# A scan whose sum trails by three units, and a quantised layer spread over more slots

## The reference

```python
deltaA = jnp.exp(delta[..., None] * A)
deltaBu = delta[..., None] * Bm[:, :, None, :] * u_bld[..., None]
h = dA * h + dBu                     # along the 512 positions
y = jnp.einsum('bdn,bn->bd', h, c)   # sum over the 16 states
```

```python
s = jnp.maximum(jnp.sqrt(jnp.maximum(amax_x, EPS) / jnp.maximum(amax_w, EPS)), EPS)
xs = x / s
ws = w * s
x_scale = jnp.maximum(jnp.max(jnp.abs(xs), axis=-1, keepdims=True), EPS) / QMAX
x_q = jnp.clip(jnp.round(xs / x_scale), -QMAX, QMAX)   # and w_q likewise
return x_q @ w_q.T * x_scale * w_scale.T
```

## Time and profile before

| what | value |
|---|---|
| median of 3 runs | 5994.26 us (5991.43 to 5997.09) |
| the profiled execution | 5995.06 us, of which the span is 5993.5 us |
| busy: PE, DVE, ACT, POOL | 4792.9, 3930.6, 2807.4, 2208.3 us |
| the scan, first recurrence to last weighing | 68.5 to 700 us |
| norm of phase 2 | 704 to 732 us |
| the eight jobs of the quantised layer | 735 to 952 us |
| phases 3 to 6 | from 953 us to the end |

### The profile page before, as it was taken

One profiled execution on the slowest core, in us unless ns is written; L12 is line 12 of the kernel. 1 busy time (PEld: TensorE's weight loads), 2 busy tenths in 40 slices (PEclk: granted clock), 3 DMA queues, 4 the chain that ended last, 5 costly groups with the idle time before them and its releaser, 6 DMA issues. The chain is left out here.

```text
span 5993.5 us, 81416 instructions
## 1 busy us (share of the span) xinstructions
PE 4792.9 (80%) x24371; PEld 3098.5 (52%) x24457; DVE 3930.6 (66%) x6523; ACT 2807.4 (47%) x5085; POOL 2208.3 (37%) x2728
## 2 busy tenths in 40 slices
PE   6788747999568888888888888888888665888857
PEld 4556534556335655655565555655655332444423
DVE  5667664322357877777777777777777244888757
ACT  5565352111034555555545555555555213777733
POOL 3455400110234554545545445455455044000100
PEclk8899877999789999999999999999999787999989
DMA  2101005244431111111111111111110044111110
GB/s 61 29 29 29 15 29 195 75 146 152 140 98 51 41 41 50 41 54 46 49 45 41 52 52 46 43 39 49 45 47 27 11 138 143 54 53 54 44 62 24
DMA packets 355942, 365.92 MB, mean 61 GB/s; under 512 B 100528, under 2 KB 253616, under 8 KB 354320
## 3 DMA queue, kind: packets, MB, share of 16 engines
q1 hardware_dynamic: 335856, 286.73, 15.9%
q0 software_dynamic: 19744, 74.99, 3.6%
HBM read 264.76 MB, written 96.86 MB: 60 GB/s over the span
## 5 line engine op out<-in xcount | busy, mean ns | idle before, releaser
L1915 POOL TENSOR_TENSOR delta_rule_suffix<-delta_rule_suffix,delta_rule_prefix 128x256 f32<-128x256 f32 x448 | 511.4, 1142 | 1088.0 <-ACT delta_rule_prefix L2016 841.2
L2300 PE MATMUL delta_rule_level<-delta_rule_qk_second,delta_rule_k_first 128*128 128x128 f32 x3072 | 444.8, 289 | 174.4 <-DVE delta_rule_L_small L2108 105.3
L2300 PEld LDWEIGHTS delta_rule_level<-delta_rule_qk_second,delta_rule_k_first 128*128 128x128 f32 x3072 | 384.4, 196 | 257.0 <-DVE delta_rule_qk_second L2119 165.2
L2276 PE MATMUL delta_rule_proj<-delta_rule_hT,delta_rule_w_qkv 128*128 128x512 f32 x1024 | 467.5, 600 | 0.0
L311 POOL TENSOR_TENSOR scan_hc<-scan_hs,scan_c_rows 128x512 f32<-128x512 f32 x256 | 334.5, 1312 | 283.6 <-DVE scan_hs L478 267.9
L2177 DVE TENSOR_TENSOR delta_rule_prefix<-delta_rule_prefix 128x256 f32<-128x256 f32 x448 | 326.5, 729 | 171.1 <-PE delta_rule_level L2288 125.9
L478 DVE TENSOR_TENSOR_SCAN scan_hs<-scan_decay,scan_inp 128x512 f32<-128x512 f32 x256 | 308.6, 1216 | 195.9 <-PE scan_inp L540 92.3
L2119 DVE TENSOR_TENSOR delta_rule_qk_second<-delta_rule_qk,delta_rule_prefix 128x512 f32<-128x512 f32 x448 | 364.7, 814 | 47.8 <-issue 12.9
L1906 POOL TENSOR_TENSOR delta_rule_k_first<-delta_rule_qk,delta_rule_suffix 128x256 f32<-128x256 f32 x384 | 304.3, 792 | 188.1 <-PE delta_rule_level L2288 160.6
L2124 DVE SCALAR_TENSOR_TENSOR delta_rule_qk<-delta_rule_proj,delta_rule_conv_w,delta_rule_qk 128x511 f32<-128x511 f32 (+2 forms) x384 | 287.5, 749 | 108.7 <-ACT delta_rule_qk L1995 84.6
L2790 DVE TENSOR_REDUCE attend_top<-attend_scores 128x1 f32<-128x512 f32 x512 | 327.7, 682 | 42.5 <-DMA delta_rule_inv_beta<-beta_dram 42.5
(11 more groups left out here) (471 smaller groups left out, 11420.6 us busy)
## 6 DMA issues: line engine op xcount, KB each, us to landing
parts_dram<-qkv_parts POOLq DMA_DIRECT2D x64, 512.0 KB, 10.5
moe_w_d<-in_w_down SPq DMA_DIRECT2D x39, 512.0 KB, 4.3
scan_c_rows<-bc_dram SPq DMA_DIRECT2D x64, 256.0 KB, 3.6
delta_rule_w_qkv<-in_kda_wq SPq DMA_DIRECT2D x64, 256.0 KB
delta_rule_w_qkv<-in_kda_wk SPq DMA_DIRECT2D x64, 256.0 KB
delta_rule_w_qkv<-in_kda_wv SPq DMA_DIRECT2D x64, 256.0 KB
delta_rule_inv_beta<-beta_dram SPq DMA_DIRECT2D x64, 256.0 KB, 3.7
delta_rule_w_o<-in_kda_wo SPq DMA_DIRECT2D x64, 256.0 KB, 4.7
```

What stands on the lines that cost most here:

```text
L1915: pool.tensor_tensor(first, first, whole_second, ALU.mult).then_inc(suffix_done, 1)
L2276: last = pe.matmul(to, w_qkv[p][:, i, k, :], hT[:, b % 2, k, :], start=(k == 0), stop=(k == DT - 1))
L2300: last = pe.matmul(level_ps[(i + 1) % 2][:, c, :], left, qk_second[:, i % 2, :, c * CHUNK // 2:(c + 1) * CHUNK // 2], start=True, stop=True)
```

## The change

The scan's `gather` trails its `feed` by three units instead of two, `turn_y` comes one unit later, and `DU_LAG` is 10 instead of 8 (for PE and ACT; POOL keeps its slot). `copy_y` and `add_y` keep theirs (n = 4 and n = 8). In the quantised layer a fourth stage is added: the output stage's slots 8 and up, run one step later. The statistics lie in slots 0 and 1, the root in 2, the inverse in 3; ACT scales the k-tiles of x one by one in slots 4 to 7, and those of w one by one in slots 0 to 3 of the next step. DVE takes off the constant, and PE and ACT turn and copy back, one part later each. The outputs move from slots 2 to 5 to slots 5 to 8, the spread product from 1 to 3, the products from 1 to 4 to 4 to 7, Silu from 4 to 7 and its product from 6 to 9. No operation is added or removed: the same instructions are issued in another order.

```diff
+    SUM_LAG = 3
...
-        ... Z_AT, Z_STEP, DU_LAG = 1, 3, 9, 18, 20, 22, 24, 6, 8
+        ... Z_AT, Z_STEP, DU_LAG = 1, 3, 9, 18, 20, 22, 24, 6, 10
...
-                        if j == Z_AT + Z_STEP * k + DU_LAG - 2:
+                        if j == Z_AT + Z_STEP * k + 6:
...
                     feed(b, j)
-                    if u >= 2:
-                        gather(*divmod(u - 2, UNITS))
-                    if n == RING + 2 and u > STATE:
+                    if u >= SUM_LAG:
+                        gather(*divmod(u - SUM_LAG, UNITS))
+                    if n == SUM_LAG + 4 and u > STATE:
                         turn_y(b * DT + k - 1)
...
-            OUT_SLOT, SILU_SLOT, ACT_SLOT, STATS_SLOT, SCALE_SLOT = 2, 4, 6, 6, 7
+            XMAX_SLOT, WMAX_SLOT, ROOT_SLOT, INVERSE_SLOT, SCALE_SLOT = 0, 1, 2, 3, 4
+            LAST_SLOT, SPREAD_SLOT, ACROSS_SLOT, PRODUCT_SLOT, OUT_SLOT, SILU_SLOT, ACT_SLOT = 1, 2, 3, 4, 5, 7, 9
...
+            def later(stage):
+
+                return lambda slot, i: stage(SLOTS + slot, i)
...
-                        if slot == STATS_SLOT:
+                        if slot == XMAX_SLOT:
                             x = hT[:, :, b * S:(b + 1) * S] if lin == 0 else actT[:, b]
                             dve.drain()
-                            dve.wait_ge(w_loaded[p], 16 * (i // 2 + 1))
                             reach(dve, w_scaled, i - 1)
                             dve.tensor_reduce(xmax[:, p, 0:n], x, AX, ALU.max, apply_absolute_value=True)
+                        elif slot == WMAX_SLOT:
+                            dve.wait_ge(w_loaded[p], 16 * (i // 2 + 1))
                             dve.tensor_reduce(wmax[:, p, 0:n], w[p][:, 0:n, :], AX, ALU.max, apply_absolute_value=True)
...
+                        elif q > 0:
+                            take_rounded(i, q - 1)
...
-                        elif slot == SCALE_SLOT:
...
+                        elif SCALE_SLOT <= slot < SCALE_SLOT + n:
+                            k = slot - SCALE_SLOT
...
+                            last = act.activation(scaled_in[p][0][:, k, :], xk, ACT.Copy, scale=unsmooth[:, p, k:k + 1])
+                            if k == n - 1:
+                                last.then_inc(x_scaled, 1)
...
-                            if q > 0:
-                                copy_turned(i, q - 1)
+                            if q > 1:
+                                copy_turned(i, q - 2)
+                        if slot < KT[JOBS[i][1]]:
+                            scale_weights(i, slot)
...
-                            if q > 0:
-                                turn_back(i, q - 1)
+                            if q > 1:
+                                turn_back(i, q - 2)
...
-                    pipeline(scales, quantize, output)
+                    pipeline(scales, quantize, output, later(output))
```

More of the change, by code:

```diff
@@ L479, in unit @@
                                            ALU.mult, ALU.add).then_inc(scanned, 1)
-                    if n == 2 * RING and u > STATE:
+                    if n == 8 and u > STATE:
                         add_y(b * DT + k - 1)
@@ L674, in output @@
                     def output(slot, i):
-                        if slot == 0:
+                        if slot == SPREAD_SLOT:
                             along = row_scale[:, i % 2, JOBS[i][1], :]
@@ L681, in output @@
                             last.then_inc(spread_done, 1)
-                    pipeline(scales, scales, output)
+                    pipeline(scales, scales, output, later(output))
                 @block.vector
@@ L732, in output @@
                         p = i % 2
-                        if OUT_SLOT <= slot < OUT_SLOT + TPB:
+                        if slot == LAST_SLOT:
+                            take_rounded(i, PARTS_OF_JOB - 1)
+                        elif OUT_SLOT <= slot < OUT_SLOT + TPB:
                             r = slot - OUT_SLOT
@@ L757, in output @@
                             dve.tensor_tensor(actT[:, b], silu[:, p], up[:, p], ALU.mult).then_inc(act_ready, 1)
-                    pipeline(stats, quantize, output)
+                    pipeline(stats, quantize, output, later(output))
                 @block.scalar
@@ L767, in scale, with scale_weights @@
                         p, n = i % 2, KT[lin]
-                        if slot == STATS_SLOT:
+                        if slot == ROOT_SLOT:
                             act.wait_ge(smooth_sq, i + 1)
                             act.activation(smooth[:, p, 0:n], smooth[:, p, 0:n], ACT.Sqrt).then_inc(smooth_root, 1)
[L771 to L782, removed]
+                        elif SCALE_SLOT <= slot < SCALE_SLOT + n:
+                            k = slot - SCALE_SLOT
+                            if k == 0:
+                                act.wait_ge(smooth_ready, i + 1)
+                                reach(act, rows_turned, PARTS_OF_JOB * (i - 1))
+                                if lin == 1:
+                                    act.wait_ge(act_ready, b + 1)
+                            xk = hT[:, k, b * S:(b + 1) * S] if lin == 0 else actT[:, b, k, :]
+                            last = act.activation(scaled_in[p][0][:, k, :], xk, ACT.Copy, scale=unsmooth[:, p, k:k + 1])
+                            if k == n - 1:
+                                last.then_inc(x_scaled, 1)
+                    def scale_weights(i, k):
+                        p, n = i % 2, KT[JOBS[i][1]]
+                        last = act.activation(scaled_in[p][1][:, k, :], w[p][:, k, :], ACT.Copy, scale=smooth[:, p, k:k + 1])
+                        if k == n - 1:
                             last.then_inc(w_scaled, 1)
@@ L809, in output @@
                         p = i % 2
-                        if slot == 1:
+                        if slot == LAST_SLOT:
+                            copy_turned(i, PARTS_OF_JOB - 2)
+                        elif slot == ACROSS_SLOT:
                             copy_turned(i, PARTS_OF_JOB - 1)
@@ L822, in output @@
                             act.activation(silu[:, p], gate[:, p], ACT.Silu).then_inc(silu_done, 1)
-                    pipeline(scale, quantize, output)
+                    pipeline(scale, quantize, output, later(output))
                 @block.tensor
@@ L860, in output @@
                         if slot == 0:
+                            turn_back(i, PARTS_OF_JOB - 2)
+                        elif slot == LAST_SLOT + 1:
                             turn_back(i, PARTS_OF_JOB - 1)
-                        elif slot == 1:
+                        elif slot == ACROSS_SLOT:
                             item = acc_item(i, 0)
@@ L868, in output @@
                             last.then_inc(acc_done, 1)
-                        if 1 <= slot < 1 + TPB:
-                            r = slot - 1
+                        if PRODUCT_SLOT <= slot < PRODUCT_SLOT + TPB:
+                            r = slot - PRODUCT_SLOT
                             item = acc_item(i, 1 + r)
```

19 lines of the change are left out of this document (11 added, 8 removed).

## The result

The changed kernel takes 5922.05 us, the median of 4 runs (5917.75 to 5929.43), against 5992.85 (4 runs): ratio 0.9885, 95% interval 0.9872 to 0.9897. That is 71 us less where 60 were forecast. The profiled execution took 5918.04 us, its span 5916.4.

What follows compares the result with a forecast made beforehand. Taken as bound: in the scan, PE, idle 81 us in waits between fixed-order queues; in the quantised layer, engines taking turns. Scan 31 (28 + 3) plus layer 29 made 60 off 5995, so 5935 us; range 5900 to 5973.

Steps and rivals of the forecast that it cites:

- The third unit: Scan: gather three units behind the feed instead of two lets PE feed one weighing earlier; 28 us less.
- each of the 43 waits can give back up to 0.87 us: Scan: one extra feed fits into each PE wait for `scan_hc`; 37 us in all, three quarters taken.
- at most 22 of the 37: Scan, around step-size chores in three batches: no order goes below 13.8 us per six units, 1.9 less each.
- DU_LAG: Scan: PE's transposes and ACT's copy of `du` two slots later; 3 us less.
- the four waits (12.7 us) all lie in batch 0: Scan: PE's waits for `du` lie where ACT's and DVE's step-size chain sets the pace; a quarter taken, 3 us.
- falls behind a switch, an Ln and two diagonals: Scan, batch 0: the first `duT` copy comes later in ACT's queue, hidden behind the first decay.
- Rival A: Scan's stalls move to DVE's waits for decays or ACT's `copy_y`; scan gives 8 us, 5958 in all; chance 0.10.
- `copy_y` at nothing: Scan: its sum comes one unit (1.75 us) later, covered by ACT's lead; costs nothing, 26 us without that cover.
- The quantised layer: Eight steps from 748.5 to 952 us: walked queue by queue, 31.6 us less, 29 taken.
- The last step's hoped 1.2 us: Quantised layer's end: 26.7 us now, walked to 25.5.
- slot 7 with Silu (5.4): Quantised layer: ACT's last element of the loop closing a full step of 26.4 us, including a 1.28 us table switch.
- What would show it: Signs expected in the later profile's scan and quantised layer, such as `scan_hc` waits below 35 us and unchanged phases 3 to 6.

Runs made afterwards that it cites:

- kernel 13: The kernel before with only ACT's copy of `du` moved from slot 9 to slot 11 of its tile; 5975.46 us, ratio 0.9972.
- kernel 9: The kernel before with the scan's sum three units behind and ACT's `du` copy at 11, PE's transposes still at 8; 5960.54 us, ratio 0.9944.
- Kernel 6: The changed kernel with x's column maximum of the next job taken in DVE's last slot of a step; 5914.20 us, ratio 0.9869.
- kernel 7: The changed kernel with ACT's Silu one slot later, at 8 instead of 7; 5924.64 us, ratio 0.9885.
- kernel 3: The kernel before with only the scan's sum three units behind, DU_LAG still 8; 5985.96 us, ratio 0.9987.
- kernel 10: The kernel before with the scan's sum three units behind and DU_LAG 11, quantised layer as before; 5946.86 us, ratio 0.9932.

## Why the prediction was right, and where it was not

- **The result** lay in the range, 13 us below the forecast. Both parts gained and no rival came in.
- **The third unit: mis-sized, 28 us forecast, 14 to 22 measured** (14.2 alone, 15.1 with ACT's copy moved, 21.6 beside all of DU_LAG 10). The step that failed is "each of the 43 waits can give back up to 0.87 us ... I take three quarters". From kernel 13 to kernel 9 PE's waits at the gather went from 46.9 to 3.5 us, and 15.1 us came of it. The gain went elsewhere than argued, too: "at most 22 of the 37" was put beside the step sizes, which gave 2.1 us in a batch; the norm and the end of the convolution gave 5.3.
- **DU_LAG: mis-sized, 3 us forecast, 21.5 measured alone and 28.9 beside the third unit**, 22.9 of it by ACT's copy. The failed step is "the four waits (12.7 us) all lie in batch 0 ... so I take a quarter". It priced the edit by PE's waits for `du` and asked nothing of ACT's copy but what its later place would delay. The cost of its early place was in the same view: 43.3 us in 14 waits. I did write that the copy "falls behind a switch, an Ln and two diagonals", and booked that as a risk; it was the gain. That PE would stop at `du` sooner with the third unit alone was right (12.7 to 30.0 us).
- **The two errors had opposite signs**, which is why the scan's sum, 31 for 43 to 45, was no further off. That is luck. The forecast's total is no evidence for its terms.
- **Rival A** rested on DVE's 69.9 us of waits for decays. 27 of them went with ACT's copy alone: they were not where stalls would move to but a second view of the same stall.
- **`copy_y` at nothing: not contradicted.** ACT's waits there did grow: of five, the one of 8.8 us behind the last decay stayed, and four went from 0.58 to 2.2 or 2.3, which is the one unit that the sum came later (11.1 us in total before, 18.0 after). Three of them lie in batch 3, which took 115.0 us against 116.0, and DVE's waits for decays fell. It was not tried by itself.
- **The quantised layer: 29 forecast, 27.5 measured.** Walked against measured: 22.1 and 23.3, 25 and 26.6, 26.4 and 26.7, 22 and 22.2, 53.1 and 52.5 for the down linear's three; ahead of it 2.2 and 1.9. The last step's hoped 1.2 us did not come: from the last job's first row maximum to the next phase it took 27.9 us before (925.3 to 953.2) and 27.9 after. Kernel 6 shows that x's column maximum is on the closing loop. The loop's last element, "slot 7 with Silu (5.4)", gave back only part of Silu's 2.3 us in each step when Silu was moved out (kernel 7); the other elements were not tried. DVE's wait for the first row maximum is 4.00 and 4.40 us at the ends of the two heaviest steps and at most 0.50 in the down linear, as said.
- **What would show it:** PE's waits for the weighed tile below 35 (4.6), batches 1 and 2 near 150 (146), batch 3 at 116 (115.0) and full steps near 26.5 (26.7) came, and phases 3 to 6 stayed within their spread; "PE's for `du` near nothing" did not (9.6 us).

## What to carry to other kernels

Price a moved instruction on every engine whose queue holds it, and from both sides: what its new place delays, and what its old place was delaying. The row to look for is a wait of the consumer that stands ahead of something another engine needs; here one number in ACT's queue gave 23 of the scan's 43 us. The total of a removed wait is a ceiling and often a poor one: 60 us of PE's waits went for 14 us of time (kernel 3 against before), and 43 for 15 with ACT's queue freed (kernel 9 against 13). And run the parts alone before believing a sum that fits.

## What was not expected of the hardware

The same instructions of the delta-rule phase took 3119.9 us in one kernel's profiled execution (kernel 10) and 3138.6 in another's (kernel 7); what decides it stays open. The switch of tables for Silu costs 1.28 us, with 0.02 us or less before it and after it, in the kernel before and after and in kernels 6, 7 and 13, also in its new place (775.46 to 776.75). The drain that the Trainium skill's page "ScalarE: Activation LUTs", section "What ACT_TABLE_LOAD costs", adds to a switch does not show: by it, some 1.4 us more would lie beside that load, and ACT is idle on neither side of it.
